# Slot mixture after linear attention: token maxima in four wide products, late weights, kv_hi on GpSimd, new orders

## The reference

```
x  = x + layernorm(attention(layernorm(x)))
x  = x + layernorm(slots(x))

attention: q = exp(x Wq'+bq), k = exp(x Wk'+bk), v = x Wv'+bv, 16 heads of 8
           kv = cumsum(k outer v), k1 = cumsum(k) along the tokens
           out = (q kv) / (q k1), then Wo', bo
slots:     xn = rmsnorm(x) gamma_x, se = rmsnorm(slot_embeds) gamma_slot (512 slots)
           logits = xn se'
           dispatch = softmax over tokens, slots = dispatch' xn
           h = gelu(slots w1), processed = h w2
           combine = softmax over slots, out = combine processed
```

## Time and profile before

| | us |
|---|---|
| median of 3 runs (lowest to highest) | 678.31 (677.71 to 678.89) |
| the profiled execution, its time | 678.04 |
| the profiled execution, its span | 676.5 |

### The profile page before, as it was taken

One profiled execution on the slowest core, in us unless ns is written; L12 is line 12 of the kernel. 1 busy time (PEld: TensorE's weight loads), 2 busy tenths in 40 slices (PEclk: granted clock), 3 DMA queues, 4 the chain that ended last, 5 costly groups with the idle time before them and its releaser, 6 DMA issues.

```text
span 676.5 us, 13340 instructions
## 1 busy us (share of the span) xinstructions
PE 608.5 (90%) x4264; PEld 533.2 (79%) x4264; DVE 472.5 (70%) x929; ACT 483.3 (71%) x1225; POOL 452.5 (67%) x466
## 2 busy tenths in 40 slices
PE   1245899999999999999999999999999999999986
PEld 0123688888888888888888888888888888888885
DVE  5455777777777777778777777777877777767631
ACT  0243678778777777877877777787787777777765
POOL 2487577777777877777777787777777777774100
PEclk9999999999999999999999999999999999999999
DMA  3000000000000000000000000000000000000000
GB/s 93 8 8 16 17 16 17 17 24 19 16 24 25 25 24 25 21 21 24 17 17 24 25 25 25 25 17 23 25 16 17 26 24 25 16 25 9 9 9 16
DMA packets 16838, 14.45 MB, mean 21 GB/s; under 512 B 2850, under 2 KB 16644, under 8 KB 16772
## 3 DMA queue, kind: packets, MB, share of 16 engines
q1 hardware_dynamic: 16772, 13.61, 6.7%
HBM read 5.25 MB, written 4.19 MB: 14 GB/s over the span
## 4 chain that ended last, share of the span: by engine, by line
PE 76%; issue 9%; DVE 7%; POOL 5%; ACT 2%; SPq 1%; DMA 1%; POOLq 0%; DVEq 0%; ACTq 0%
PE HB L684 16%; PE LA L695 8%; PE HB L545 5%; PE HB L547 4%; PE HB L546 4%; PE LA L650 4%; PE LB L659 4%; PE LA L668 3%; DVE slots L921 3%; PE WB L604 3%; PE HB L676 3%; PE WB L545 2%; PE LB L547 2%; PE LB L546 2%; PE LB L545 2%
## 5 line engine op out<-in xcount | busy, mean ns | idle before, releaser
L848 DVE TENSOR_TENSOR prod<-WB,E 128x1024 f32<-128x1024 f32 (+1 forms) x96 | 91.2, 950 | 65.4 <-PE WB L622 65.4
L684 PEld LDWEIGHTS HB<-w_c,hid 128*128 128x128 f32 x1024 | 123.2, 192 | 3.7 <-issue 1.2
L684 PE MATMUL HB<-w_c,hid 128*128 128x128 f32 x1024 | 124.5, 275 | 0.8 <-ACT hid L397 0.8
L314 POOL TENSOR_TENSOR kv_lo<-kv,kv_hi 128x1152 fp32r<-128x1152 f32 x32 | 86.1, 2691 | 51.7 <-ACT kv_hi L390 51.7
L397 ACT ACTIVATE hid<-HB 128x512 f32<-128x512 f32 x128 | 76.3, 596 | 8.4 <-PE HB L547 2.2
L864 DVE TENSOR_REDUCE numden<-prod 128x288 f32<-128x2304 f32 x32 | 81.4, 2543 | 0.0
L306 POOL TENSOR_TENSOR kv<-E 128x1024 f32<-128x1024 f32 x32 | 68.3, 2133 | 18.5 <-ACT E L390 18.3
L390 ACT ACTIVATE disp<-LA 128x512 f32<-128x512 f32 x64 | 34.9, 595 | 62.8 <-PE LA L650 62.7
L361 POOL TENSOR_TENSOR kv<-kv,kv_prev 128x1024 f32<-128x1024 f32 x32 | 76.7, 2397 | 0.0
L306 POOL TENSOR_TENSOR kv_prev<-prev 128x1024 f32<-128x1024 f32 x32 | 68.3, 2136 | 0.1
L668 PE MATMUL LA<-xn,disp 128*128 128x128 f32 x512 | 64.7, 280 | 0.1
(11 more groups left out here) (133 smaller groups left out, 1566.7 us busy)
## 6 DMA issues: line engine op xcount, KB each, us to landing
X<-in_L_attn_x_dram SPq DMA_DIRECT2D x32, 128.0 KB, 2.0
out_dram<-res SPq DMA_DIRECT2D x32, 128.0 KB, 1.9
prev<-E SPq DMA_DIRECT2D x32, 112.0 KB, 2.1
w_in<-in_L_ffn_w_dram SPq DMA_DIRECT2D x2, 256.0 KB, 3.4
prev<-E SPq DMA_DIRECT2D x32, 15.0 KB, 2.1
se_in<-n_L_ffn_slot_embeds_dram SPq DMA_DIRECT2D x1, 256.0 KB, 2.9
w_in<-in_L_attn_Wq_dram SPq DMA_DIRECT2D x1, 64.0 KB, 1.8
w_in<-in_L_attn_Wk_dram SPq DMA_DIRECT2D x1, 64.0 KB, 2.2
```

The lines of the kernel that those rows point to most:

```text
L314: pool.tensor_tensor(kv_lo[:, :], kv[:, :], kv_hi[:, :].bitcast(F32), ALU.subtract)\
L684: last = pe.matmul(PR[:, j, :], hid[:, f, j * P:(j + 1) * P], w2_c[:, f, :], start=(f == 0), stop=(f == FJ - 1))
L848: dve.tensor_tensor(prod[:, :, d0 * DIM:d1 * DIM].rearrange("p c (d f) -> p c d f", d=g), WB[:, k % 2, 0:g * DIM].rearrange("p (o d f) -> ...
```

## The change

- `subtract_max` makes four products of 256 columns (two slot tiles g at once, the negative identity read twice) in place of eight of 128.
- xn gets a 129th column of ones, so `gather_slots` also gives the sums of the dispatch weights; `dispatch_exp` has no accumulator any more, and `slots_scale` takes the reciprocal of the gathered sums. SL and OB lie in both banks of LA.
- `sums_high` moves from ScalarE to GpSimd as a `tensor_copy` of 1152 columns. prod has two buffers.
- x[0] is loaded first on SyncE, ScalarE's queue issues the loads of the biases and of wo, slot embeddings, gammas, w1 and w2. Only wq, wk, wv are prepared before the pipeline; the rest (`slot_squares`, `slot_norms`, `slot_scale`, `slot_transpose`, `slot_parts`, `wo_order`, `wo_transpose`, `wo_centre`, `bo_centre`, `w1_parts`, `w2_centre`) is done inside the first steps, once, for batch 0.
- The steps of all engines are reordered. Some calls only move over the step's edge (their batch changes with them).

```diff
-                for j in range(SJ):
+                for g in range(2):
                     for c in range(NC):
-                        last = pe.matmul(LBv[:, j, c * P:(c + 1) * P], tok_max[:, c:c + 1].broadcast_to((P, P)),
-                                         neg_ident[:, :], start=False, stop=True, skip_group_check=True)
+                        last = pe.matmul(LBv[:, 2 * g:2 * g + 2, c * P:(c + 1) * P],
+                                         tok_max[:, c:c + 1].broadcast_to((P, P)),
+                                         neg_ident[:, :].rearrange("p (o t) -> p o t", o=1).broadcast_to((P, 2, P)),
+                                         start=False, stop=True, skip_group_check=True)
...
-                        last = pe.matmul(SL[:, j, :], disp[:, c, j * P:(j + 1) * P], xn[n % 2][:, c, :],
+                        last = pe.matmul(SL[:, j // 2, j % 2, :], disp[:, c, j * P:(j + 1) * P], xn[n % 2][:, c, :],
...
             def slots_scale(n):
-                after(dve, disp_exp, n)
-                dve.reciprocal(disp_inv[:, :], disp_sum[:, :]).then_inc(slots_inv, 1)
+                after(dve, slots_done, n)
+                dve.reciprocal(disp_inv[:, :].rearrange("p (g j) -> p g j", g=2), SL[:, :, :, DIM]).then_inc(slots_inv, 1)
...
+            def sums_high(n):
+                after(pool, kv_built, n)
+                after(pool, kv_den, n)
+                after(pool, cum_done[UN - 1], n - 1)
+                pool.tensor_copy(kv_hi[:, :], kv[:, :]).then_inc(kv_hi_ready, 1)
```

More of the change, by code:

```diff
@@ L114, in attention_and_slot_mixture @@
         own = [sb(f"own{u}", [P, HD + 1, NH]) for u in range(2)]
-        prod = sb("prod", [P, NC, FEAT])
+        prod = [sb(f"prod{u}", [P, NC, FEAT]) for u in range(2)]
         numden = sb("numden", [P, NC, HD + 1, NH])
@@ L363, in step @@
             def step(z, a, b, l, r, t, p, q, w):
+                if r is not None:
+                    own_value(r, r % 2)
                 if t is not None:
+                    pair_sum(t)
+                    sums_high(t)
+                if p is not None:
+                    slot_norms(p)
+                if t is not None:
+                    own_product(t, t % 2)
                     sums_low(t)
@@ L379, in step @@
                     x1_rstd_of(r)
[L380 to L383, removed]
             pipeline(pool, step)
@@ L699, in step @@
             def step(z, a, b, l, r, t, p, q, w):
+                if a is not None:
+                    mixture(a, a % 2)
+                if l is not None:
+                    xn_transpose(l)
+                if b is not None:
+                    hidden(b)
+                if p is not None:
+                    x_transpose(p)
+                if l is not None:
+                    logits(l)
+                if t is not None:
+                    slot_transpose(t)
                 if r is not None:
@@ L939, in step @@
             def step(z, a, b, l, r, t, p, q, w):
+                if b is not None:
+                    slots_scale(b)
+                if r is not None:
+                    multiply(r, r % 2, 1)
+                if l is not None:
+                    x1_normalise(l, l % 2)
+                if r is not None:
+                    wo_centre(r)
+                    own_sum(r, r % 2)
+                if b is not None:
+                    slT_low(b)
+                if r is not None:
+                    multiply(r, r % 2, 2)
+                if p is not None:
+                    slot_squares(p)
+                if l is not None:
+                    xnT_low(l)
+                if r is not None:
+                    attention(r, r % 2)
                 if p is not None:
                     xT_low(p)
+                if t is not None:
+                    slot_scale(t)
                 if l is not None:
```

331 lines of the change are left out of this document (173 added, 158 removed).

## The result

The changed kernel takes 719.04 us (median of 4 runs, 717.01 to 719.88) beside 678.60 us of the kernel before (4 runs, 677.71 to 678.91): the ratio is 1.059, 95% interval 1.057 to 1.062, slower. The forecast was 708 with a range of 692 to 738. The profiled execution took 718.82 us, its span 717.1.

The account below looks back on a forecast made before the run. It took a ring of waits through TensorE, 18.81 us a period, as the bound. 678.0 + 38.6 (29 steps of 1.33, att held) - 8.5 (start, fill, drain) = 708, range 692 to 738.

Parts of the forecast that it names:

- The mechanism: VectorE's att (two SBUF inputs) stands until GpSimd's kv_lo ends, plus 0.28 us, so the attention transpose starts late; 0.77.
- The ring's segments: Four stretches of one period, slots to slots through TensorE's attention transpose and gather: 18.81 us before, 18.84 + K after.
- K: Duration of the new kv_hi copy (128x1152) on GpSimd; taken as 1.3 us, with 1.1 or 2.1 from other rows.
- TensorE's idle time before the attention transpose: TensorE was to stand idle some 2.3 us before each attention transpose, released by att.
- Start and fill: First project at 10.2, 12.6 us sooner; 6 us come back in the fill from prepared work and held att.
- att's hold in the two fill steps: VectorE's att, held in the first two steps, was to add 3.1 and 0.6 us to the fill.
- The drain: The last two steps have no kv_lo and were to gain 0.94 us each, -1.9 in all.
- The gain of 1.15 us between dispatch transpose and gather: Ten TensorE instructions were to move behind the gather, cutting attention transpose to gather from 8.71 to 7.56 us.
- Rival (a): att slips in ahead of kv_lo, or a hole remains: period 17.87, 639 us; chance 0.17 shared with (c).
- (b): TensorE's 256-column products cost what two did, adding up to 0.46 us a period: 722 us with the hold; chance 0.04.
- (c): GpSimd's work is the bound without a hold, 17.7 to 17.9 us a period: 639 to 645; 0.17 shared with Rival (a).
- (d): Gains and hold cancel, leaving the time the same; needs K of 0.26; chance 0.02.

Follow-up runs that it names:

- the one wait: Against the changed kernel, GpSimd's kv_lo of a batch waits until att of the batch before is written; 647.63 us, ratio 0.955.
- the accumulators: The changed kernel with kv_lo waiting for att, and dispatch sums from ScalarE's accumulator again, reciprocal taken before the wait for the gather; 642.45 us, ratio 0.948.
- own_product late: The changed kernel with own_product moved on GpSimd from between kv_hi and kv_lo to behind x_rstd; 716.82 us, ratio 1.057.
- eight products: The changed kernel with kv_lo waiting for att, and eight 128-column products back in place of four of 256; 654.26 us.

## Why the prediction was right, and what it had wrong

**The mechanism held.** att is caught by kv_lo and ends 0.28 after it. The ring's segments, forecast and measured: slots to own_sum 2.25 and 2.37; own_sum to attention transpose 6.7 + K and 7.86, with K measured at 1.15 so 7.85; attention transpose to gather 7.56 and 7.63; gather to slots 2.32 and 2.21. They add up to 18.84 + K = 19.99, measured 20.07. Shown by taking it away: the one wait brings 71 us (0.955), and bringing it alone into the kernel before costs 88.

**K was mis-sized.** 1.3 taken, 1.15 measured, inside the bounds of 1.1 and 2.1: 29 x 0.15 = 4 us too much. That att is held didn't depend on K, only the time at which it is released did. L927 was forecast inside kv_hi (K over 1.2); with K under 1.2 it fell into own_product, as the forecast says for that case. Held there, it passed att on later, so att stood 2.36 in a steady period (mean 2.34) where some 3 was forecast.

**The term that was missing: +12.3 us.** The sum counted TensorE's idle time before the attention transpose (2.3 forecast, 2.0 measured) at its own length. It costs more: in eight of 28 periods the clock fell to 1.2 GHz after it, 1.5 us each. The range of the forecast was built from K and the fill and set nothing aside for this. The rest of the 10.7 us between forecast and profile (708.1 and 718.8) nearly cancels: K 4 us too much, the other segments 2 too little, start and fill 2 too much, the last steps 2 too little. So with the idle time filled, 706.5 lies near the 708 in part by luck.

**Start and fill.** Project at 10.02 (10.2 forecast), with slots first at -8.7 in place of -12.6 + 6 = -6.6. For att's hold in the two fill steps the sum added 3.1 + 0.6; its first two rows are 0.86 and 2.74 us, beside 0.43 and 2.43 before, so it grew by 0.4 and 0.3 only.

**The drain was wrong.** The last two steps were to gain 0.94 each; they took 17.24 and 17.04, beside 17.09 and 16.71 before. TensorE's timeline there:

```profile
694.36 1.09 PE L673 MATMUL LA<-ident,disp_t 128*128 128x128 f32 x8 [2.24 <-ACT disp_t L467]
```

The dispatch transpose now stands ahead of half of process, so in steps with little else on TensorE it waits for ScalarE's exponentials, which process used to cover.

**A step that was wrong and cost nothing.** The gain of 1.15 us between dispatch transpose and gather was put down to TensorE's instructions; the four products alone brought nothing, and with TensorE's new order added the kernel lost 34 us. Only with ScalarE's order changed too did it gain.

**The rivals.** Rival (a) came true nowhere in this kernel, and its price was good: with att ahead of kv_lo and L927 free the period is 17.91 (17.87 forecast) and the time 643 (639). (b) is refuted: from the first product to what follows, four wide ones take 0.55 us and eight narrow ones 0.92, which is 0.37 of the 0.46. Within their group the wide ones start every 0.118 us (median of 96) and the narrow ones of the kernel before every 0.112. By the Trainium skill (PSUM — Partial Sum Buffer, Specifications) any non-contiguous pattern slows matmuls significantly. The trace doesn't show it for this pattern: the contiguous products of 256 columns into LB start every 0.117 us too. (The 722 that the forecast names for (b) is 721 by its own terms, 708 + 13.) (c) GpSimd is no bound: with the wait it stands 33.8 us before kv_lo alone, and the kernel is faster. (d) needed a K of 0.26.

**What stays open.** What decides in which periods the clock falls: the idle time before it is 1.9 to 2.05 us in periods with and without a lapse, and moving own_product, which shortened the idle time to 1.6 us and the period with it, made lapses more frequent (13 of 28). TensorE's and ScalarE's new orders with the early start and nothing else wasn't run; kv_hi back on ScalarE in the kernel after has them together with the new orders of VectorE and GpSimd, and its period is 18.18, not 17.94, for which no run gives the reason. The best one measured is the change with the wait for att and the accumulators, 642.45 us, 5.2% under the kernel before (0.948, 0.945 to 0.950).

## What to carry to other kernels

Before an operation goes to GpSimd because another engine is busy, lay GpSimd's timeline over VectorE's: an idle gap there may be what lets a two-input VectorE instruction on the critical ring through, and one wait that makes GpSimd stand back can be worth more than the time it gives up. A reordering belongs to all engines at once: the same lines moved on TensorE cost 5% with ScalarE's old order and brought 3% with a new one. And when two edits each bring 0.2 us, run them together before naming a cause for either.

## What the runs showed of the hardware

- **A VectorE instruction with two inputs in SBUF stands until the GpSimd instruction that it meets has ended.** att, issued in the midst of kv_lo, ended 0.28 to 0.29 us after it in each of 26 periods of the four kernels with the hold; L868 ended 0.16 us after the copy of kv_hi (0.156 to 0.168 in the kernel before with kv_hi on GpSimd). Issued in the last 0.1 us of that copy it took its usual 0.31 us (own_product late without the wait).
- **The hold goes both ways, and hundredths decide.** L927 and own_product start almost together in nearly every steady period of the kernel after and of the run with the wait alone. Where L927 starts up to 0.03 us after own_product it takes 0.60 to 0.62 us and own_product its 0.46; where it starts 0.01 to 0.02 us ahead it takes its 0.31 and own_product 0.61 or 0.62; where it starts 0.07 to 0.11 us ahead (with eight products, and with the accumulators), own_product takes 0.52 to 0.56. The one that starts first makes the other wait.
- **A copy of one input on GpSimd holds as well** (L868 0.70 us in place of 0.31, kv_hi alone on GpSimd), and 1152 elements from fp32 to fp32r take 1.15 us there, 1.16 on ScalarE.
- **TensorE's clock can fall to 1.2 GHz in an otherwise busy kernel.** It did so in 8 of 28 periods of the kernel after, each time after TensorE had stood 1.9 to 2.05 us for att, at 1.5 us each; in 13 of 28 with 1.6 us (own_product late) and in 12 of 28 with 2.2 us (kv_hi alone). With 0.41 us idle in its place no steady period of that profile was over 20.29.
